# Scaling the gathered rows on ACT in the four-head attention pass of a graph network

## The reference

```python
def _gat_layer(x, src, dst, W, a_src, a_dst, b, heads, out_dim):
    h = (x @ W).reshape(n, heads, out_dim)
    al_s = jnp.einsum('nhd,hd->nh', h, a_src)
    al_d = jnp.einsum('nhd,hd->nh', h, a_dst)
    e = jax.nn.leaky_relu(al_s[src] + al_d[dst], SLOPE)
    m = jax.ops.segment_max(e, dst, num_segments=n)
    p = jnp.exp(e - m[dst])
    denom = jax.ops.segment_sum(p, dst, num_segments=n) + 1e-16
    w = p / denom[dst]
    msg = h[src] * w[:, :, None]
    out = jax.ops.segment_sum(msg, dst, num_segments=n)
    return out.reshape(n, heads * out_dim) + b
```

## Time and profile before

| | us |
|---|---|
| median of three timed runs | 18431.7 (18422.38 to 18434.54) |
| the profiled execution, its span | 21138.5 |
| PE busy in it | 9540.9 |
| DVE busy | 8097.6 |
| ACT busy | 1416.9 |
| POOL busy | 12654.5 |

### The profile page before, as it was taken

One profiled execution on the slowest core, in us unless ns is written; L12 is line 12 of the kernel. 1 busy time (PEld: TensorE's weight loads), 2 busy tenths in 40 slices (PEclk: granted clock), 3 DMA queues, 4 the chain that ended last, 5 costly groups with the idle time before them and its releaser, 6 DMA issues. The chain is left out here.

```text
span 21138.5 us, 217919 instructions
## 1 busy us (share of the span) xinstructions
PE 9540.9 (45%) x37741; PEld 7773.1 (37%) x37741; DVE 8097.6 (38%) x29032; ACT 1416.9 (7%) x3852; POOL 12654.5 (60%) x12031
## 2 busy tenths in 40 slices
PE   0333333322222278888888885333333333333334
PEld 0222222222222266666666663232322332223233
DVE  6344444343434533333333334333333333543334
ACT  0000000000000111111111111000000000000000
POOL 1555555355555268888888882666646666356665
PEclk6555555555555566666666667555555555555556
DMA  2321221311111255555555553111121111111111
GB/s 70 57 48 48 48 48 46 48 38 40 38 39 38 62 108 106 106 106 106 106 106 106 106 105 95 44 44 44 44 68 44 44 44 44 40 51 44 44 44 48
DMA packets 1753968, 1328.70 MB, mean 63 GB/s; under 512 B 528762, under 2 KB 1576227, under 8 KB 1750312
## 3 DMA queue, kind: packets, MB, share of 16 engines
q0 software_dynamic: 570240, 778.48, 18.2%
q1 hardware_dynamic: 1182704, 530.37, 10.0%
q10 hardware_dynamic: 728, 17.33, 0.2%
HBM read 1134.48 MB, written 230.11 MB: 65 GB/s over the span
## 5 line engine op out<-in xcount | busy, mean ns | idle before, releaser
L692 POOL DMA_INDIRECT wk<-tab,idx x4992 | 4782.6, 958 | 3237.1 <-ACT idx L682 1767.1
L704 PE MATMUL PS<-wk 128*128 128x128 f32 x9984 | 2731.3, 445 | 4889.3 <-DVE wk L716 3724.4
L854 POOL DMA_INDIRECT hs<-tab_g,wk x3328 | 3232.1, 971 | 2663.0 <-ACT wk L815 1650.2
L704 PEld LDWEIGHTS PS<-wk 128*128 128x128 f32 x9984 | 2241.0, 319 | 5380.3 <-DVE F L726 3232.2
L1471 POOL DMA_INDIRECT agg<-F x1664 | 2632.9, 1582 | 515.0 <-issue 505.2
L918 PE MATMUL PS<-wk,hs 128*128 128x128 f32 x6656 | 1628.7, 416 | 2738.3 <-DVE wk L939 1302.6
L726 DVE TENSOR_TENSOR F<-F,PS 128x128 f32 x4992 | 1442.5, 289 | 3638.0 <-issue 1626.0
L918 PEld LDWEIGHTS PS<-wk,hs 128*128 128x128 f32 x6656 | 1379.9, 302 | 2991.3 <-DVE wk L939 1348.3
L1460 POOL DMA_INDIRECT F<-tab,idx x1664 | 1642.9, 987 | 720.5 <-issue 487.5
L960 DVE TENSOR_TENSOR F<-F,PS 128x126 f32 x3328 | 952.0, 286 | 2310.0 <-issue 1773.6
L716 DVE TENSOR_SCALAR wk<-iota_row,locT 128x128 f32<-128x128 f32 x4992 | 1240.2, 304 | 1154.0 <-issue 1120.2
(11 more groups left out here) (287 smaller groups left out, 8190.1 us busy)
## 6 DMA issues: line engine op xcount, KB each, us to landing
F<-src_d SPq DMA_DIRECT2D x416, 256.0 KB
F<-loc_rows_d SPq DMA_DIRECT2D x416, 256.0 KB
F<-tab_b SPq DMA_DIRECT2D x1664, 64.0 KB
wk<-tab,idx POOLq DMA_INDIRECT x4992
hs<-tab_g,wk POOLq DMA_INDIRECT x3328
F<-tab,idx POOLq DMA_INDIRECT x1664
agg<-F POOLq DMA_INDIRECT x1664
F<-agg SPq DMA_DIRECT2D x56, 448.0 KB
```

The lines of the kernel that those rows point to most:

```text
L692: pool.indirect_dma_start(gbuf[j], None, table, bass.IndirectOffsetOnAxis(idx[:, j:j + 1], 0))\
L704: pe.matmul(bank(j % 8, P), gbuf[j], onehot[j], start=True, stop=True).then_inc(summed.sem, 1)
L854: pool.indirect_dma_start(gt[s][:, j, :], None, table, bass.IndirectOffsetOnAxis(bidx[s][:, j:j + 1], 0))\
```

## The change

In the pass with four heads, DVE's `scale(h)` goes. ACT gets a `scale(h)` of its own: for each block four `activation` instructions (Identity, scale from a column of `w_c`) of 128 x 32, one for each head, in place, with the signal `scaled` on the last of the four. They are issued for quarters 0 and 1 right after `w_ready`, for quarter 2 ahead of the wait for `summed` of quarter 1, and for quarter 3 ahead of that of quarter 2. DVE keeps its one-hots and adds in their order. The pass with one head is as it was.

```diff
                             act.wait_ge(w_turned.sem, w_turned.after(n + 1))
                             act.copy(w_c[:, 0:R], bank(6, R)).then_inc(w_ready.sem, 1)
+
+                            def scale(h):
+
+                                act.wait_ge(w_ready.sem, w_ready.after(n + 1))
+                                for j in range(h * HALF, (h + 1) * HALF):
+                                    for e in range(heads):
+                                        part = gt[s][:, j, e * (D // heads):(e + 1) * (D // heads)]
+                                        last = act.activation(part, part, ACT.Identity, scale=w_c[:, e * BT + j:e * BT + j + 1])
+                                    last.then_inc(scaled.sem, 1)
+
+                            if heads > 1:
+                                scale(0)
+                                scale(1)
                             for h in range(QH):
                                 q = n * QH + h
+                                if heads > 1 and 0 < h < QH - 1:
+                                    scale(h + 1)
 
                                 act.wait_ge(summed.sem, summed.after(q + 1))
...
-                            def scale(h):
-                                for j in range(h * HALF, (h + 1) * HALF):
-                                    g3 = gt[s][:, j, 0:D].rearrange("p (h d) -> p h d", h=heads)
-                                    w3 = heads_of(w_c)[:, :, j:j + 1].broadcast_to([P, heads, D // heads])
-                                    v.tensor_tensor(g3, g3, w3, ALU.mult).then_inc(scaled.sem, 1)
-
...
-                            if heads > 1:
-                                scale(0)
-                                scale(1)
-                            else:
+                            if heads == 1:
                                 onehots(0)
                                 onehots(1)
                             for h in range(2, QH):
                                 add(h - 2)
                                 onehots(h)
-                                if heads > 1:
-                                    scale(h)
                             add(QH - 2)
                             add(QH - 1)
```

## The result

| | before | after |
|---|---|---|
| median, us | 18427.3 (18422.38 to 18434.54, 4 runs) | 18543.83 (18541.79 to 18547.1, 4 runs) |
| ratio to before, 95% interval | | 1.0062 (1.0048 to 1.0077) |
| profiled execution, us | 21138.5 | 18540.1 |

The change makes the kernel 0.6% slower, by 116 us. The forecast was 18740, by 308 us: the right sign, but 2.6 times the size. In a later comparison, run `e12`, the same kernel took 18534.51 us beside 18415.33, 1.0064 (1.0049 to 1.0080).

The account below looks back on a forecast made before the run. POOL's gather pace was taken to bound the four-head pass at 41.2 us a tile; the new ACT and DVE loop of 47.1 us adds 5.9 us x 52 = 308 us, 18431.7 + 308 = 18740 us, range 18640 to 18850.

Parts of the forecast that it names:

- The thinned-out profile is an effect of the profiling: Slow instruction starts during POOL's gathers, taken as profiling only: 2832.8 us of waits against 2706.8 us of extra profiled time.
- POOL's pace, 41.2 us a tile: Four-head pass before: 32 gathers at 0.981 us plus 0.305 us between two, taken as the bound of the timed runs.
- DVE's scalings are worth nothing: Taking 6.6 us a tile of scalings off DVE gains nothing as such, its chain having 6 us of room.
- Rival B: Faster: short ACT slot, and POOL gains what DVE gives up, 0.9 us a tile, 48 us in all: 18384; chance 0.05.
- The ACTIVATE slot: Distance between starts of ACT's new 128 x 32 scalings: 0.22 us, times 128 = 28.2 us a tile.
- Rivals A and D: A: slot 0.12 to 0.17 us, time stays 18432, chance 0.12. D: no overlap, slot 0.32, 19404, chance 0.06.
- The loop through ACT and DVE: Last scaling, copy, DVE's last adds, next softmax and its scalings run one after the other: 47.1 us a tile.
- The loop heads: DVE loses 2.8 us at each of 25; ACT's like loss hidden beside DVE's adds, costed at nothing, uncovered 70 us.
- Rival E: Identity and Exp don't share ACT's table: two loads a tile add 133 us, 18873; chance 0.04.
- Rival C: Some thinning out stays in timed runs beside gathers: 2 to 5 us a tile more, 18844 to 19000; chance 0.15.
- The lower end of the range: 18640 us, named for a slot of 0.205 us and a tile of 42.4 us now; range's chance 0.58.

Follow-up runs that it names:

- e12: The changed kernel measured again with no edit: 18534.51 us beside 18415.33 for the kernel before, 1.0064.
- e1: The kernel before, unedited, profiled again without thinned-out stretches: 18441.42 us beside 18440.24, 1.000.
- e11: The kernel before, with DVE's scaling reading the weights from the PSUM bank instead of the SBUF copy w_c: 18259.24 us beside 18415.33, 0.9915.
- e13: The changed kernel, last quarter's scaling cut in two with the copy of quarter 2 between: 18448.96 us beside 18416.81 for the kernel before, 1.0017.
- e14: The kernel before plus 20 more tensor_tensor a tile on DVE, two SBUF inputs each, into scratch: 18616.63 us beside 18416.81, 1.0107.

## Why the prediction was wrong, step by step

**The thinned-out profile is an effect of the profiling: wrong.** The timed runs of before took 21165.16 and 21296.77 us in two comparisons. What sets the condition stays open; it isn't the chip alone, for two chips each showed both. The sum that led there (POOL's loop waits of 2832.8 us are what the timed runs lack) was sound as arithmetic, and its conclusion held: `e1` shows POOL bound by its own pace. The cause that I put under it was not shown by it.

**POOL's pace, 41.2 us a tile: the step that failed.** It measured 43.5 (`e1`). I took the mean of 0.981 us from a profile in which POOL didn't gather while DVE scaled quarters 2 and 3. Two rows of the first profile of before, not used in the prediction, show it:

```profile
2006.72 0.95 POOL L854 DMA_INDIRECT hs<-tab_g,wk  x1 [0.30 <-issue]
...
2024.81 0.96 POOL L854 DMA_INDIRECT hs<-tab_g,wk  x1 [17.14 <-ACT wk L815]
```

The scalings of quarters 2 and 3, at 2013.59 and 6.4 us later, fell into POOL's idle 17 us; of the 98 bursts of eight in that profile 97 met no gather. In the measured condition POOL never idles, and they meet its gathers. The scalings' price on POOL is (1.054 - 0.963) x 32 = 2.9 us a tile, and only (0.981 - 0.963) x 32 = 0.6 of it was in the sum. So the old tile was 2.3 us too short, 2.3 x 52 = 120 us too much in the forecast.

**DVE's scalings are worth nothing: wrong for the same reason.** As DVE time they are, with 6 us of room. As what they do to POOL they were the whole distance from the steady tile of `e11`, 40.6 us, to 43.5. Rival B named the mechanism (POOL gains what DVE gives up), but priced it at 0.9 us from the mean of the wrong profile, and let it act only if ACT's chain stayed short. It acts in any case; here the new loop swallows it.

**The ACTIVATE slot: 0.22 predicted, 0.212 measured**, 0.309 us long against 0.320. 27.1 us a tile in place of 28.2. The estimate from the Trainium skill ("ScalarE: Activation LUTs", What ACT_TABLE_LOAD costs), 0.213 and 27.3, was the better one. Rivals A and D are refuted by the slot.

**The loop through ACT and DVE: the path was right, the size 1.5 us too long.** 47.1 us predicted, 45.6 measured. 1.1 us of it is the slot; the copies between the scalings, which I put at 0.5 us, took 0.1. Without its scalings the loop is 45.6 - 27.1 = 18.5 us against 18.9. `e13` shows that the adds belong to it. 1.5 x 52 = 78 us too much.

**The loop heads: right.** DVE still loses time there, 68.4 us over 25 heads. ACT now loses 63.1, 2.5 us each, beside DVE's adds and at no cost that shows in the sum. Rival E is refuted: ACT still loads its table once per two tiles.

**Rival C** gives too much time as well; nothing of the thinning out is in the comparison that counts.

**The lower end of the range** was worked out wrongly. 18640 is named for a slot of 0.205 us and a tile of 42.4 us now; the slot alone gives 18637, both together give (18.9 + 26.2 - 42.4) x 52 = 142 us and 18574. The measured 18543.83 lies under that too.

The forecast, put right with the two terms: 52 x (45.6 - 43.5) = 109 us. The first interval, where the gathers and the computing of a tile come one after the other, adds 78.1 - 69.6 less these 2.1 us, 6 us. That makes 115, where 116 were measured. The sign came out right by a narrow margin: with the measured terms the change would have broken even at a slot of (43.5 - 18.5) / 128 = 0.195 us, worked out and not run.

POOL's own gain is real in the profile after: 0.965 us a gather, POOL waiting 260.2 us for ACT. The prediction had expected more than 872 us of such waits and a pass longer by over 308 us, both for a thinned-out profile, which this one wasn't.

## What to carry to other kernels

Before a duration from a profile becomes a pace, compare the profile's span with the timed runs; if they differ, a mean may come from stretches in which the engines overlapped otherwise, and what an operation does to its neighbours is lost with it. Where POOL issues gathers all the time, look for DVE instructions with both inputs in SBUF: here they cost POOL's time as well as DVE's, and the longer the unbroken row, the longer the gather waited. An operand that is in PSUM anyway (here the weights, which ACT had only copied out) can be read there; here that took 156 us off. Whether pauses in the row would do as well wasn't run. A mean over a pass's tiles also holds its first, which overlaps with nothing; leave it out when a steady loop was summed. Four short ACTIVATE for one wide DVE instruction cost four slots, and whatever waits behind them in ACT's order joins the loop.

## What the runs showed of the hardware

- A POOL gather that meets eight back-to-back SBUF and SBUF `tensor_tensor` took 2.49 us in place of 0.96; with one input in PSUM 0.96. One-hots by `tensor_scalar` from SBUF to SBUF didn't hold it up (0.96), nor did ACTIVATE (mean 0.965).
- A gather that was held up ended 0.82 to 0.85 us after the last instruction of the unbroken row, for rows of 8, 13, 16 and 26 (269 gathers of `e1` and `e14`).
- An ACTIVATE of 128x32 with a per-partition scale takes 0.309 us and starts every 0.212 us.
- The same kernel ran at 18415 to 18440 us in some comparisons and at 21165 to 21297 in others, with many instructions of ACT, DVE and PE started 0.7 or 1.4 us apart or more in the later part of POOL's gathers. Two chips each ran in both ways. No run here shows what brings it about.
